# Starting to pick after one prepared tile instead of seven, in a graph-aggregation kernel

## The reference

```python
mask = A != 0
scores = jnp.where(mask, -jnp.arange(N), -inf)
vals, idx = jax.lax.top_k(scores, 25)
feats = jax.vmap(lambda x, i: x[i])(X, idx)
feats = jnp.where((vals > -inf)[..., None], feats, -inf)
agg = feats.max(axis=2)
degree = mask.sum(axis=-1)
agg = jnp.where((degree <= 25)[..., None], jnp.maximum(agg, 0.0), agg)
h = jnp.concatenate([X, agg], axis=-1)
out = jax.nn.relu(jnp.einsum('bnf,fo->bno', h, W) + b)
x = layernorm(x + out)
```

## Time and profile before

| | |
|---|---|
| median of three runs | 624.4 us |
| the profiled execution | 624.25 us, of which 622.4 us are the span |
| TensorE busy | 501.3 us (81%) |
| VectorE busy | 534.3 us (86%) |
| ScalarE busy | 394.6 us (63%) |
| GpSimd busy | 290.4 us (47%) |
| adjacency read | 56 loads of 512 KB, and 8 for tile 0 |

### The profile page before, as it was taken

One profiled execution on the slowest core, in us unless ns is written; L12 is line 12 of the kernel. 1 busy time (PEld: TensorE's weight loads), 2 busy tenths in 40 slices (PEclk: granted clock), 3 DMA queues, 4 the chain that ended last, 5 costly groups with the idle time before them and its releaser, 6 DMA issues.

```text
span 622.4 us, 14481 instructions
## 1 busy us (share of the span) xinstructions
PE 501.3 (81%) x4480; PEld 341.9 (55%) x4544; DVE 534.3 (86%) x973; ACT 394.6 (63%) x751; POOL 290.4 (47%) x462
## 2 busy tenths in 40 slices
PE   1366997889968996889974999679987999779982
PEld 0124675566654675456752666555764567555762
DVE  4656999899898998899995998998898999998884
ACT  3361577448965688557864588665886478545744
POOL 2643365246633655146733356335552467336610
PEclk9997999899998999799997999998999999899996
DMA  8982336353434647345534445355544463021102
GB/s 244 224 221 72 102 98 129 98 153 96 134 95 137 151 115 125 106 130 143 132 97 112 133 107 137 86 141 137 135 124 120 116 141 59 18 57 36 46 10 70
DMA packets 91815, 71.38 MB, mean 115 GB/s; under 512 B 63651, under 2 KB 80294, under 8 KB 91686
## 3 DMA queue, kind: packets, MB, share of 16 engines
q1 hardware_dynamic: 85286, 56.77, 35.6%
q0 software_dynamic: 6400, 13.12, 8.4%
HBM read 50.99 MB, written 4.19 MB: 89 GB/s over the span
## 4 chain that ended last, share of the span: by engine, by line
PE 30%; DVE 22%; issue 14%; ACT 12%; DVEq 8%; DMA 7%; another core or an unknown queue 3%; POOL 1%; SPq 1%; POOLq 1%; ACTq 0%
PE pair L1037 25%; DVE part L776 11%; DMA adj_sb<-in_adj 3%; ACT row_work L712 3%; DMA g_feat<-in_x,g_idx 3%; DVE hot L771 3%; ACT mask L586 3%; DVEq L846 3%; DVEq L915 2%; ACT distance L629 2%; ACT hot L636 2%; DVE g_feat L849 2%; PE misc L1082 1%; DVE g_val L817 1%
## 5 line engine op out<-in xcount | busy, mean ns | idle before, releaser
L1037 PE MATMUL pair<-hot,x_part 128*128 128x128 bf16 (+3 forms) x3120 | 416.6, 281 | 66.0 <-DVE part L776 33.8
L1037 PEld LDWEIGHTS pair<-hot,x_part 128*128 128x128 bf16 x3120 | 239.0, 99 | 176.1 <-issue 64.0
L776 DVE TENSOR_REDUCE part<-pair 128x128 f32<-128x1024 f32 (+1 forms) x256 | 279.8, 1099 | 47.2 <-PE pair L1037 45.9
L484 POOL DMA_INDIRECT g_feat<-in_x,g_idx x200 | 192.8, 964 | 112.5 <-issue 96.0
L521 POOL TENSOR_TENSOR y_sb<-relu_sb,x_sb 128x128 f32<-128x128 f32 x64 | 32.8, 512 | 194.1 <-ACT relu_sb L647 193.8
L593 ACT ACTIVATE V<-p_V 128x512 bf16<-128x512 f32 x98 | 58.0, 592 | 93.4 <-remote 71.7
L621 ACT ACTIVATE hot<-V,first_bias 128x1024 bf16<-128x1024 bf16 x56 | 64.1, 1145 | 52.8 <-PE pair L1037 52.8
L771 DVE TENSOR_SCALAR hot<-V 128x1024 bf16<-128x1024 bf16 x224 | 84.3, 397 | 0.0
L586 ACT ACTIVATE mask<-adj_sb 128x1024 bf16<-128x1024 uint32 x56 | 58.8, 1050 | 20.5 <-DMA adj_sb<-in_adj 20.5
L636 ACT ACTIVATE hot<-distance,one 128x1024 bf16<-128x1024 bf16 x56 | 64.0, 1143 | 0.2
L629 ACT ACTIVATE distance<-V,second_bias 128x1024 bf16<-128x1024 bf16 x56 | 63.7, 1137 | 0.0
(11 more groups left out here) (88 smaller groups left out, 396.6 us busy)
## 6 DMA issues: line engine op xcount, KB each, us to landing
adj_sb<-in_adj SPq DMA_DIRECT2D x56, 512.0 KB
g_adj<-in_adj SPq DMA_DIRECT2D x8, 512.0 KB, 4.4
x_sb<-in_x SPq DMA_DIRECT2D x8, 512.0 KB, 3.9
out<-y_sb SPq DMA_DIRECT2D x7, 512.0 KB, 5.1
g_feat<-in_x,g_idx POOLq DMA_INDIRECT x200
maskT<-mask SPq DMA_TRANSPOSE x56
out<-y_sb SPq DMA_DIRECT2D x1, 448.0 KB, 3.0
w_sb<-in_W SPq DMA_DIRECT2D x1, 128.0 KB, 6.3
```

The source lines that it names most:

```text
L484: pool.indirect_dma_start(out=g_feat[w][:, k, :], out_offset=None, in_=x_rows, in_offset=bass.IndirectOffsetOnAxis(ap=g_idx[w][:, k:k + 1] ...
L776: dve.tensor_reduce(part[:, par(q, s), :, p], slots_of(q, s, p).rearrange("f k i -> f i k"), AX.X, ALU.max).then_inc(s_used, 1)
L1037: last = pe.matmul(dst, x_part[:, q, part_no, kb], one_hot, start=(first and part_no == 0), stop=(final and part_no == PARTS - 1))
```

## The change

The prologue prepares tile 1 of the first batch alone. `to_prepare` then gives the steps of the first batch two tiles each: step 1 prepares tiles 2 and 3, step 2 tiles 4 and 5, step 3 tiles 6 and 7, step 4 tiles 1 and 2 of the second batch, and so on, and step 7 the last one. From the second batch on, one tile is prepared per step as before. With it:

- the levels of the first batch are found in three passes (`levels_at`: tiles 1 and 2 in step 1, 3 to 5 in step 3, 6 and 7 in step 4), since the counts are not there earlier;
- the three first extraction steps of tile 0 stay in the prologue, the others go into steps 1 and 2 (`FIRST_STEPS`), and the gathers into steps 3 to 5, nine at a time (`gather0`);
- the second and third part of the first `x` are computed by VectorE, in one instruction each;
- SP loads `x` and turns the first mask before it loads tile 2's adjacency.

Cut to its core:

```diff
+        def to_prepare(i, q, s):
+            if is_first(i, q):
+                return [(0, n // MT, n % MT + 1) for n in (2 * s - 1, 2 * s) if n < 2 * MT]
+            t = ahead(i, q, s, FRONT)
+            return [t] if t else []
+        def levels_at(i, q, s):
+            return ({1: (1, 2), 3: (3, 5), 4: (6, MT)} if is_first(i, q) else {1: (1, MT)}).get(s)
@@ SP @@
             load_adj0(0, 0)
             load_adj(0, 0, 1)
+            load_x(0, 0)
+            transpose_mask(0, 0, 1)
             load_adj(0, 0, 2)
-            load_x(0, 0)
...
-            transpose_mask(0, 0, 1)
-            for n in range(2, FRONT + 3):
...
+            load_adj(0, 0, 3)
+            transpose_mask(0, 0, 2)
+            load_adj(0, 0, 4)
@@ GpSimd, gather0 @@
-                if s == 1:
+                first, each = (3, -(-K // 3)) if is_first(i, q) else (1, GATHER)
+                if s == first:
...
@@ ScalarE, step @@
+                    early = is_first(i, q) and s == 1
+                    if early:
+                        copy_V(*a, 0)
+                        copy_V(*a, 1)
...
-                    if to_rank:
-                        copy_V(*to_rank, 1)
+                    if b:
+                        copy_V(*b, 0)
+                        copy_V(*b, 1)
+                        make_mask(*ahead(*b, 2))
+                    elif a:
+                        copy_V(*a, 1)
                     if s > 1:
                         relu(i, q, s - 1)
@@ VectorE @@
+            FIRST_EXTRACT = {1: {}, 2: {2: 0}, 3: {0: 1, 2: 2}, 4: {0: 3, 2: 4}, 5: {0: 5, 2: 6}, 6: {}, 7: {1: 7, 2: 8}}
+            FIRST_STEPS = {(1, 0): 3, (1, 1): 4, (1, 2): 5, (1, 3): 6, (1, 4): 7, (2, 0): 8}
...
-                        if s == 1 and p == 1:
-                            count_violations(i, q)
+                        if levels_at(i, q, s) and p == 1:
+                            count_violations(i, q, s)
...
-                        if s == 1 and p == COUNT[s] - 2:
-                            set_levels(i, q)
+                        if levels_at(i, q, s) and p == (COUNT[s] - 2 if s == 1 else 1):
+                            set_levels(i, q, s)
+            for st in range(3):
...
+            dve.tensor_tensor(x_rest[:, :, :], x_sb[:, 0], x_part[:, 0, 0], ALU.subtract).then_inc(s_rest, NT)
+            dve.tensor_copy(V[:, 0, 0, BANK:2 * BANK], pairs[1][:, BANK:2 * BANK]).then_inc(s_V, 1)
+            dve.tensor_tensor(x_part[:, 0, 2], x_rest[:, :, :], x_part[:, 0, 1], ALU.subtract).then_inc(s_split, NT)
             one_hots(0, 0, 1, range(ACT_RANKS, DEPTHS[1][0]))
@@ TensorE, step @@
                     pick_group(i, q, s, 1)
-                    if s > 1 and to_rank:
-                        out_free(i, q, ORDER[s - 1])
-                        count(*to_rank)
+                    if b:
+                        rank_product(*a, 1)
+                    if a and (begin or s > 1) and not levels_now:
+                        out_free(i, q, ORDER[s - 1] if s > 1 else 0)
+                        count(*a)
                     pick_group(i, q, s, 2)
+                    if levels_now:
+                        violations(i, q, s)
+                        pe.wait_ge(s_level, level_pass(i, q, s))
...
+                    if b:
+                        rank_product(*b, 1)
...
+                    if b:
+                        out_free(i, q, ORDER[s])
+                        count(*b)
```

More of the change, by code:

```diff
@@ L929, in step @@
                     nxt = (i, q, s + 1) if s < MT else None if last else (ni, nq, 1)
-                    steps = {} if last else EXTRACT[s]
+                    steps = {} if last else FIRST_EXTRACT[s] if begin else EXTRACT[s]
                     gaps = COUNT[s] - 1
@@ L1026, in count @@
                 if s == 1 and not (isinstance(n, int) and n < 1):
[L1027 removed]
+                    pe.wait_ge(s_viol, 2 * i + q + 2)
                 pe.wait_ge(s_mT[par(q, s)], 16 * nth(i, q, s))
@@ L1121, in step @@
                     if s in (*TURNS, MT):
-                        pe.wait_ge(s_V, copied - 1 if to_rank else copied)
+                        pe.wait_ge(s_V, copied - 1 if a and not b else copied)
                     if s in TURNS:
```

177 lines of the change are left out of this document (87 added, 90 removed).

## The result

The changed kernel took 641.85 us (median of 4 runs, 637.90 to 645.72), the kernel before 624.95 in runs beside it: a ratio of 1.0265, 95% interval 1.0192 to 1.0338. It is slower, as forecast, and by more than twice as much. The profiled execution, 637.90 (span 635.9, mean clock 0.940), is the third shortest of the 16 and 13.65 above the profiled one of before; it shows less of the loss than most runs have.

What follows compares the result with a forecast made beforehand. Prologue bound by a chain of waits, steps 2 to 7 by nearly full TensorE and VectorE; -19.6 + 4.2 + 16.8 + 6.8 - 5.4 = +2.8, plus 4.3 for the clock, +7.1 on 624.25: 631 us, range 619 to 638.

Steps and rivals of the forecast that it cites:

- The start: Prologue: first pick at 18.4 instead of 38.05, a gain of 19.6 us (18.6 with a load of 5.0).
- Step 1: First batch: four more extraction operations on VectorE between the groups, a loss of 4.2 us, bounds 3.6 and 4.8.
- The ends of steps 2 to 6: First batch: TensorE's last count waits for ScalarE's relu, 2.5 us more per step; with half products and copies 16.8 together.
- The copies' waits: Ends of steps 4 to 6: a copy between the second tile's two half products, 0.7 us more each, 2.1 in all.
- the half products: Steps 2 to 6: two further half products cost TensorE 0.22 us each, raising the loss per step from 2.5 to 2.9.
- The level: Steps 3 and 4: TensorE waits for VectorE's level, 3.6 and 3.2 to 3.6 us; loss 6.8, bounds 0 and 7.2.
- Step 7: First batch: VectorE's backlog and slow products go, a gain of 5.4 us from 15.9, bounds 2.9 and 5.8.
- The gathers: GpSimd, first batch: 39 us from step 2's relu to landing, costing nothing as long as the steps are long.
- The clock, first batch: TensorE's new waits bring half-clock stretches of 1.43 us each; three of none to seven taken, a loss of 4.3.
- The rule that I cited as a rival: First batch: every wait brings the slow clock, seven stretches of 1.43 us, 637 us in total; chance 0.11.
- this shift goes through to the end: Second batch on: engines' order is unchanged, so the second batch's shift from 118.74 carries to the end.
- from there on the distances of before: Sign to look for: second batch at 122 to 128 instead of 118.74, the distances after it unchanged.

Runs made afterwards that it cites:

- e1: Changed kernel with ScalarE doing the relu before the second tile's copies and mask in steps 2 to 6 of the first batch: 627.89 us, ratio 1.0054.
- e6: Kernel before with the changed first batch's gathers, 9, 9 and 7 in steps 3 to 5: 631.11 us, ratio 1.0132.
- e0: Changed kernel run again, unedited: 642.81 us, ratio 1.0271.
- e9: Changed kernel with nops meant to pad GpSimd's program; they are not in the compiled program, so a mere repeat: 641.84 us.
- e3: Kernel before with eight chained, unused copies of x on ScalarE ahead of its first one-hots, as a delay: 629.68 us, ratio 1.0089.
- e4: Changed kernel with SyncE's first transfers back in the order of the kernel before: 638.99 us, ratio 1.0265.
- e16: Changed kernel with 246 semaphore increments inside a branch of TensorE's first step that isn't taken: 638.01 us, ratio 1.0206.
- e15: e7 with 246 semaphore increments inside a branch of TensorE's first step that isn't taken: 621.37 us, ratio 0.9926 against the kernel before.
- e7: Changed kernel with e1's relu move and TensorE's fourth group of steps 3 and 4 ahead of the violations product: 625.39 us, ratio 1.0008.
- e10: Kernel before with 10 increments of an unused semaphore at the start of TensorE's program: 626.87 us, ratio 1.003.
- e12: Kernel before with 10, 25 and 13 semaphore increments on TensorE, VectorE and ScalarE: 624.96 us, ratio 1.0008.
- e11: Changed kernel with 246 executed semaphore increments at the start of TensorE's program: 663.18 us, ratio 1.0628.

## Why the prediction was near for the first batch and wrong behind it

- **The start.** 18.52 against 18.4: right to 0.1 us.
- **Step 1.** It took 25.2, 2.3 more than in before, not 4.2. The extraction operations are there, but the second round of products took 4.23 at 37.63 (granted clock 0.65 over it) where before had 5.30 (0.50). The row of before, from which the prediction also took the idle 3.12 that it ascribes to the earlier trace rows:

```profile
53.83 5.30 PE L1037 MATMUL pair<-hotx,x_part 128*128 128x256 bf16 x24 [3.12 <-DVE hotx L783]
```

- **The ends of steps 2 to 6.** Waits of 2.02 and four times 1.80, and 1.0 instead of 0.25 at the restart: 2.5 to 2.8 more each, against 2.5. That it was the relu, e1 shows. The copies' waits are 0.91 in steps 4 to 6, against 0.7; the half products are as worked out.
- **The level.** 3.50 in step 3 (2.33 and 1.17) as forecast, 1.82 in step 4, where VectorE was further ahead: 5.3 against 6.8.
- **Step 7.** 11.6 instead of 15.9: 4.3 against 5.4.
- **The gathers** cost nothing in the first batch, as said; e6 shows that in steps as short as those of before they would.
- **The clock, first batch.** The terms as they came sum to: -19.5 + 2.3 + steps 2 to 6 (72.2 against 41.9) 30.3 - 4.3 = +8.8. Of the 30.3, end waits with restarts 13.2, half products 2.2, copies 2.7 and level 5.3 are 23.4, and 6.9 is left. I put it down to work at the lower clock, where I took 4.3. The changed kernel after its wait for the level, TensorE:

```profile
63.52 0.34 PE L1059 MATMUL misc<-ones_bf,maskT 128*128 128x1 bf16 x8 [1.17 <-DVE level L932]
...
65.76 3.58 PE L1065 MATMUL pair<-hot,x_part 128*128 128x512 bf16 x21
```

and the window over it, columns as in the earlier trace rows:

```profile
64.00:68.00 4.00, 4.00 (x24) 2.52 (x23) 1.68 (x4) 0.60 (x1) 2.83 (x3) 0.57 0.50 115
```

Up to here the profiled execution is 1.7 us off (8.8 against 7.1). That is nearer than the terms were: step 1, the level and step 7 were off by 1.9, 1.5 and 1.1 us, the ends and the clock by 1.3 and 2.6, and these in part cancel. Other executions of the same program lost more: marks of 135.3 (e0) and 135.9 (e9) instead of 133.0, and a granted clock of 0.88 in e0's first 130 us where this one had 0.93. Read by windows of 2 us, the first batch has two slow stretches in before (the second round and step 7) and five in the profiled execution of the changed kernel, one of them again the second round. Of the seven places that the prediction had in mind (two waits for the level, five ends of steps), four were slow in this execution, five in e9 and six in e0, and three was too few in each. The rule that I cited as a rival (the Trainium skill, TensorE: Matmul & The Clock Gate, section on the second failure mode, psum-queue depth-cycling) would, carried through, make all seven slow; so for e0 it was nearer than my count, though no execution had all seven.

- **The step that failed** is "and this shift goes through to the end", with its sign to look for, "from there on the distances of before". The sum put nothing there, since the order of instructions is the same from the second batch on; but the time isn't: rest 502.9, 506.8 and 506.8 in the three profiles of the changed program against 498.2 and 501.1 in two of before, 4.7 to 8.6 us more than the first of these. The mark, too, came 8.8 to 11.7 later, where 7.1 had been summed, and there it is the clock term that was sized too small. e3 speaks against the delay as the cause of the longer rest, e4 and e6 against the transfers' order and the first batch's gathers. e16 took 4 us off by medians, by moving TensorE's program alone without changing what runs, and e15 against e7 took 4 again. What stands in the step's place: the change put ten instructions ahead of the later batches, so a piece of program is fetched over the last gather of a batch, VectorE's wait for it grows, and with it the batch.

What stays open: the place's price differs (4 in e16 and e15, 2.1 in e10, nothing in e12), and the pieces of q14 are not tied to an engine's program. With the place restored, e16 is still 13 above before, and in its profile all of that lies ahead of the mark (15.2 later, rest 0.5 shorter), at a mean granted clock of 0.88 up to there against 0.95 in before: the lower clock comes and goes between executions. Of 91 runs of before, from 618.7 to 629.9 us (one more, of 2028 us, is left out), those with more of it took longer. The time at the lower clock, reckoned as 2 x (1 - mean clock) x span, was 53.6 us on average, and each microsecond of it went with 0.20 us more time. In the changed program it was 85. By the slopes of 0.20 to 0.30 found within before and within the changed program, these 31 us go with 6 to 9 of the 17.5. That is a correlation; no run held everything else fixed.

## What to carry to other kernels

When work is moved into a loop's tail, look at what the other engine has queued ahead of the one short instruction that this tail waits for: moving one relu of 0.27 us ahead of 2 us of copies and a mask gave back 15 of 17.5 us, some of it, it seems, by way of the clock. Two engines that were nearly full lost more by a few new waits per step than the twenty microseconds of earlier start had gained: each wait costs itself, its restart, and often a stretch at half clock. And where instructions are added ahead of a loop, "the same order" is not yet the same time: compare the landings of the transfers that end a wait, before trusting that a shift goes through.

## What the runs showed of the hardware

- The place of TensorE's program in its packets of 16 KB (q8) decided which transfer a fetch met. Ten instructions of 64 bytes moved the fifth fetch of the second batch from 46.1 to 43.7 us after the mark, and the landing of that batch's last gather from 1.60 to 1.72 us (eight profiles) to 2.37 to 2.95 (nine). Increments in a branch that isn't taken moved it back, with nothing added to the rest (497.7 in e16).
- When a piece of program started behind the issue of a batch's last gather, the landing came a nearly fixed time behind the piece: 1.63 to 1.65 us behind one of q14 (27 cases), 2.1 to 2.6 behind one of q8 (25).
- A semaphore increment on TensorE took some 105 ns (246 of them delayed it by 25.8 us in e11, although it had idle time there).
- After the wait for a relu the counts on TensorE took 0.35 us, but the next group came 1.0 us behind them ("issue"), against 0.25 to 0.31 at the ends of steps where TensorE hadn't waited.
- The same program varied from 618.7 to 629.9 us over 91 runs, with mean granted clocks of 0.967 and 0.948 at these ends.
